# FFN weight differences in the heads of grouped attention, three running sums of probabilities, and denominators placed ahead of the natural-order turn

## The chip, the core and the metric

The program runs on one core of a Trainium2 chip. The core has five engines that run side by side, each in its own order: TensorE (PE, matmuls; PEld is its weight load), VectorE (DVE), ScalarE (ACT), GpSimd (POOL) and SyncE (SP), which here only issues DMAs. They wait for one another through counters (semaphores). The metric is the device time of one execution in microseconds (us). Three runs of the kernel before took 909.49, 909.55 and 912.41 us, so the median is 909.55 us.

## The reference

A perceiver layer on 8 batches of 64 tokens of 512 features (512 tokens in all), in three parts, each added to x:

```python
x = x + xattn(layernorm(x), ctx)   # 16 heads of 32, 1601 context rows per batch, softmax over them
x = x + attn(layernorm(x), ...)    # 32 query heads of 128 in 8 groups of 4, 576 keys, softmax
x = x + ffn(layernorm(x), ...)     # gate and up 512 -> 1792, silu(gate) * up, down 1792 -> 512

def _binary_diff_weight(w, base):  # each of the three FFN weights
    d = w - base
    coeff = jnp.mean(jnp.abs(d))   # one number over all 512 x 1792 elements
    return base + coeff * jnp.sign(d)
```

The mean of |w - base| needs all of w and all of base before the first FFN weight can be made. The change concerns where in the program this mean is gathered.

## The kernel before

**Cross attention** runs over 8 batches `b`. The 1601 context rows are 13 tiles `t` of 128 (the last has 65 rows). In the loop for batch `b`, PE makes scores of batch `b`, the unnormalised values `u` from the exponentials (`values(b, u)`, two tiles at a time), and beside them the scores of batch `b + 1` from which DVE takes row maxima (`max_scores`, `take_max`). ACT makes the exponentials in four buffers `probs`. The denominator of the softmax is the sum of the exponentials over all 13 tiles: POOL adds tiles in pairs into six buffers `sums` (`add_pair`, `add_tail`, seven additions), and PE multiplies the six buffers by a block of ones (`denominators`, twelve matmuls of 512 columns in three rounds of four). At the end of a batch PE's order is: compress the context of batch `b + 3`, turn the maxima, the last `values`, `natural(b + 3)` (a transpose), two score tiles of the next batch, `denominators(b)`. ACT copies the denominators (`copy_den(b - 1)`) after tile 1 of the next batch and before tile 2. In the same loop POOL subtracts three blocks of FFN weights of 896 columns per batch (`difference`) and ACT sums their magnitudes (`abs_sum`, in the array of that name), fed by `load_pieces` on SP's queue. 24 blocks cover all three weight pairs.

**Keys and new tokens** (`rotated_keys`) come next and are not touched.

**Grouped attention** (`attention_and_ffn`) runs 32 heads, `n = 4 g + i`. Heads of groups 1 to 6 stand in a hardware loop. In the pass of head `n`, every engine does this head's scores and exponentials, and the second half of head `n - 1`: PE turns its probabilities (`turn_probs`), ACT copies them to `probs_t_high`, DVE makes `probs_t_low`, PE multiplies by the values (`mix`, which raises `pv`), ACT copies the product to `mixed_t_high`, DVE makes `mixed_t_low` (raises `al`). POOL multiplies each of the head's four probability tiles by the inverse denominator. In the first head of a group (`i = 0`) POOL also waits for `pv` and copies the group's values, and PE runs `output`, 48 matmuls that need `mixed_t_low` from the tenth on. SP loads in each pass the query weight for four heads on, after `wql`, and the output weight for four heads on, after `wol`, which DVE raises in `output_weight_low`. For a group's first head, DVE does `output_weight_low(g, 0)` only in the pass of the second head (`if i == 1`).

**FFN** follows. Before the first head, PE adds the sums over partitions and DVE makes `coeff`; the weights are quantised from the last group on.

The pass of a head, as ACT and DVE have it, and SP's loop stand in full below, with all other functions that the change touches.

## Time and profile before

| | |
|---|---|
| median of 3 runs | 909.55 us |
| the profiled execution | 912.59 us, of it the span of 910.7 us that the profile shows |
| cross attention | 0 to about 295 us |
| keys and new tokens | about 295 to 325 us |
| 32 heads | about 325 to 780 us |
| FFN | about 780 to 911 us |
| PE busy | 866.1 us (95%) |
| DVE, ACT, POOL busy | 609.3, 521.5, 416.2 us |

A timeline row reads: start, duration, engine, line, operation, output<-input with shape, count, and in brackets how long the engine stood idle before it and what released it. Rows that touch in time are merged, so "x4" is four instructions in one row. A matmul's duration contains its way through the array; consecutive ones overlap. A row of windows reads: stretch, its length, then for PE, PEld, DVE, ACT and POOL the busy time and the number of instructions, then the granted clock of TensorE as a share of 2.4 GHz, the busy share of the DMA engines and GB/s.

### The profile page before, as it was taken

The page shows a single profiled execution, that of the slowest core. Times are in us where ns is not written, and L with a number is a line of the kernel's source. Part 1 is how long each engine was busy: PE and PEld are TensorE (multiplying, and loading weights), DVE is VectorE, ACT ScalarE, POOL GpSimd, SP SyncE. Part 2 cuts the span into 40 slices and gives each one's busy share as a digit, 9 for nine tenths or more (in the row PEclk, how much of TensorE's full clock was granted, in tenths as well). Part 3 has the DMA queues.
Part 4 walks back from the last instruction along what each step waited for, and adds up shares of the span by engine and source line. Part 5 has one row for each costly group of instructions (what it writes and reads, how often), then busy time and mean ns, then how long its engine had stood idle before and what let it go on. Part 6 is the DMA issues. An engine that isn't in the chain of part 4 may idle for free.

```text
span 910.7 us, 15512 instructions
## 1 busy us (share of the span) xinstructions
PE 866.1 (95%) x5402; PEld 656.5 (72%) x5402; DVE 609.3 (67%) x994; ACT 521.5 (57%) x1010; POOL 416.2 (46%) x272
## 2 busy tenths in 40 slices
PE   6789999999997989999999999999999999899998
PEld 4444555455442668888888888888888887788886
DVE  4665666576551538858587585876858769768884
ACT  4555666666674547636366373763637647555552
POOL 2397887788876015424244242442424524154430
PEclk9979999999998889999999999999999999999999
DMA  9747664623660721102011020110202003445531
GB/s 365 273 173 290 234 244 145 257 89 113 186 202 1 277 82 47 47 1 70 23 46 46 0 69 23 48 44 8 72 12 67 14 1 113 165 139 189 197 101 47
DMA packets 43202, 102.96 MB, mean 113 GB/s; under 512 B 7954, under 2 KB 13074, under 8 KB 42258
## 3 DMA queue, kind: packets, MB, share of 16 engines
q1 hardware_dynamic: 42866, 102.06, 32.6%
q8 instruction: 30, 0.49, 0.2%
q10 hardware_dynamic: 288, 0.26, 0.1%
q14 instruction: 18, 0.15, 0.1%
HBM read 96.95 MB, written 1.05 MB: 108 GB/s over the span
## 4 chain that ended last, share of the span: by engine, by line
PE 60%; DVE 2%; ACT 1%; DMA 1%; POOL 0%; SPq 0%; issue 0%
PE psum L1356 11%; PE psum L1342 10%; PE psum L1472 8%; PE psum L1410 8%; PE psum L1368 6%; PE psum L1486 4%; PE psum L1395 3%; PE psum L1386 3%; PE psum L1391 3%; PE psum L1377 1%; PE psum L1387 1%; PE psum L1389 1%; DMA ffn_raw<-in_L_ffn_mean_w_dram 1%; POOL ffn_quant L1857 0%; DVE x L1828 0%; DVE norm_stats L162 0%
## 5 line engine op out<-in xcount | busy, mean ns | idle before, releaser
L1844 POOL TENSOR_TENSOR head_probs<-head_probs,inverse_den 128x576 f32<-128x576 f32 x128 | 147.3, 1151 | 273.2 <-DVE inverse_den L1697 273.1
L979 DVE TENSOR_REDUCE max_part<-psum 128x1 f32<-128x804 f32 x128 | 121.2, 990 | 48.3 <-PE psum L693 48.2
L869 ACT ACTIVATE probs<-psum 128x512 f32<-128x512 f32 (+1 forms) x208 | 107.8, 601 | 56.5 <-PE psum L714 48.6
L1579 ACT ACTIVATE head_probs<-psum,neg_max 128x576 f32<-128x576 f32 x128 | 94.7, 740 | 51.2 <-DVE neg_max L1710 50.4
L555 POOL TENSOR_TENSOR prob_sums<-probs 128x1024 f32<-128x1024 f32 x48 | 114.0, 2383 | 19.5 <-ACT probs L869 10.5
L1710 DVE TENSOR_REDUCE neg_max<-psum 128x1 f32<-128x576 f32 x128 | 96.9, 757 | 23.9 <-PE psum L1356 22.7
L1356 PE MATMUL psum<-k_high,query_t_high 128*128 (+1 forms) x256 | 86.7, 339 | 2.0 <-DVE coeff L1783 2.0
L1690 DVE TENSOR_TENSOR probs_t_low<-psum,probs_t_high 128x512 fp32r<-128x512 f32 x124 | 84.8, 684 | 1.0
L714 PE MATMUL psum<-q_t,c_t 97*128 97x512 f32 (+1 forms) x208 | 74.2, 437 | 8.7 <-ACT probs L869 7.0
L693 PEld LDWEIGHTS psum<-c_t,q_t 96*128 96x128 f32 x256 | 43.9, 191 | 50.9 <-DVE max_part L979 29.3
L693 PE MATMUL psum<-c_t,q_t 96*128 96x402 f32 x256 | 75.0, 376 | 5.6 <-DVE max_part L979 3.9
L1368 PE MATMUL psum<-ident,head_probs 128*128 128x128 f32 x496 | 77.9, 273 | 1.6 <-DVE query_t_low L1669 1.4
L1857 POOL TENSOR_TENSOR ffn_quant<-ffn_raw 128x1536 f32<-128x1536 f32 x13 | 45.6, 3508 | 67.6 <-DVE ffn_w_low L1774 26.9
L1356 PE MATMUL psum<-k_high,query_t_low 128*128 (+1 forms) x256 | 76.2, 298 | 0.0
L1356 PE MATMUL psum<-k_low,query_t_high 128*128 (+1 forms) x256 | 76.1, 297 | 0.0
L1585 ACT ACTIVATE probs_t_high<-psum 128x512 fp32r<-128x512 f32 x124 | 72.9, 588 | 0.5 <-PE psum L1377 0.5
L1368 PEld LDWEIGHTS psum<-ident,head_probs 128*128 128x128 f32 x496 | 60.6, 140 | 11.4 <-issue 2.2
L714 PEld LDWEIGHTS psum<-q_t,c_t 97*128 97x128 f32 (+1 forms) x208 | 38.4, 192 | 32.1 <-ACT probs L869 23.0
L1593 ACT ACTIVATE wo_t_high<-wo_nat 128x512 fp32r<-128x512 f32 x32 | 20.0, 626 | 72.4 <-PE psum L1410 72.4
L727 PE MATMUL psum<-probs,c_nat 128*32 128x512 f32 (+1 forms) x416 | 61.0, 621 | 0.0
L1752 DVE TENSOR_TENSOR x<-psum,x 128x512 f32<-128x512 f32 x32 | 22.1, 690 | 46.0 <-PE psum L1410 46.0
L548 POOL TENSOR_TENSOR w_raw<-w_raw 128x896 f32<-128x896 f32 x24 | 50.5, 2105 | 4.3 <-DMA w_raw<-in_L_ffn_mean_w_dram 4.3
(221 smaller groups left out, 1924.3 us busy)
## 6 DMA issues: line engine op xcount, KB each, us to landing
ctx_t_odd<-in_ctx_dram SPq DMA_DIRECT2D x4, 3202.0 KB, 10.7
w_raw<-in_L_ffn_w_dram SPq DMA_DIRECT2D x24, 448.0 KB, 5.3
w_raw<-in_L_ffn_mean_w_dram SPq DMA_DIRECT2D x24, 448.0 KB, 6.4
ffn_raw<-in_L_ffn_w_dram SPq DMA_DIRECT2D x42, 256.0 KB, 3.9
ffn_raw<-in_L_ffn_mean_w_dram SPq DMA_DIRECT2D x42, 256.0 KB, 4.2
cache<-in_ctx_dram SPq DMA_DIRECT2D x3, 3202.0 KB, 10.6
wq_nat<-in_L_attn_wq_dram SPq DMA_DIRECT2D x32, 256.0 KB, 2.9
wo_nat<-in_L_attn_wo_dram SPq DMA_DIRECT2D x32, 256.0 KB, 2.7
```

Source lines behind the costliest of these rows:

```text
L555: pool.tensor_tensor(sums[u][:, :], prob_buffer(b, 2 * u)[:, :], prob_buffer(b, 2 * u + 1)[:, :], ALU.add).then_inc(s_add, 1)
L693: mm = pe.matmul(psum[:, bank + k, 0:PIECE_KEYS], q_t[0:SHIFT, b, 2 * qt:2 * qt + 2, :].rearrange("p h n -> p (h n)"), c_t[0:SHIFT, b % 3, ...
L714: pe.matmul(psum[0:rows_of(t), n % SCORE_BANKS, :], lhs, rhs[:, half * BANK:(half + 1) * BANK], start=True, stop=True).then_inc(s_sb, 1)
L869: act.activation(prob_buffer(b, t)[0:rows, half * BANK:(half + 1) * BANK], psum[0:rows, n % SCORE_BANKS, :], ACT.Exp, scale=XSCALE).then_i ...
L979: dve.tensor_reduce(max_part[:, qt, pair:pair + 1], psum[:, bank:bank + 2, 0:PIECE_KEYS], AX.XY, ALU.max).then_inc(s_max, 1)
L1342: mm = pe.matmul(psum[:, head_bank(i), :], wq_t[a][:, c, :], (xh, xl)[b][:, c, :], start=(k == 0), stop=(k == 3 * DC - 1))
L1356: mm = pe.matmul(psum[:, bank, 0:HALF], q_t[a][:, qt * P:(qt + 1) * P], (k_high, k_low)[b][:, keys], start=(step == 0), stop=(step == 2))
L1368: mm = pe.transpose(bank[:, t * P:(t + 1) * P], probs[:, qt, t * P:(t + 1) * P], core.ident[:, :])
L1579: act.activation(probs[:, qt, :].rearrange("p (a k) -> p a k", a=2), psum[:, 2 * (qt % 2):2 * (qt % 2) + 2, 0:HALF], ACT.Exp, bias=neg_max ...
L1690: dve.tensor_tensor(probs_t[1][:, 0:ST, qt * P:(qt + 1) * P], psum[:, turn_bank(qt), :].rearrange("p (t q) -> p t q", t=ST), probs_t[0][:, ...
L1710: dve.tensor_reduce(neg_max[:, qt:qt + 1], psum[:, 2 * (qt % 2):2 * (qt % 2) + 2, 0:HALF], AX.XY, ALU.max, negate=True).then_inc(s["max"], 1)
L1844: pool.tensor_tensor(probs[:, qt, :], probs[:, qt, :], rden[:, qt:qt + 1].to_broadcast([P, KEYS]), ALU.mult).then_inc(s["norm"], 1)
```

## The change

Three things move.

1. **The FFN weight blocks leave cross attention.** `load_pieces`, `difference` and `abs_sum` are gone from it. In grouped attention the weights are cut into 28 pieces of 256 columns, one per head of the first seven groups. In pass `n` SP first waits for `s_abs >= 3n + 1`, issues the six DMAs of piece `n` (`load_piece`) and only then goes to the query weight and the output weight. POOL, after the head's four tiles (and in `i = 0` after the values), adds the last piece's three sums to `total`, waits for all six DMAs, and subtracts the blocks in the order 1, 2, 0. ACT sums the magnitudes of blocks 1 and 2 in the same pass, ahead of the copy to `mixed_t_high`, and those of block 0 in the next pass, ahead of the first exponential. `coeff` is made in head 28 and no longer before head 0.
2. **Three running sums in cross attention.** POOL adds tile by tile into three buffers (tiles 0 to 3, 4 to 7, 8 to 12), ten additions for a batch in place of seven; two sets alternate between batches.
3. **`denominators` takes the place of the last `values`**, ahead of `natural(b + 3)` and the next batch's scores. It holds the last tile's two value matmuls and six matmuls of the sums (twelve before), the last four of them after POOL's last addition.

```diff
-PIECE = WSIZE // P // BATCH
+PIECE = WSIZE // P // (NH - REP)
...
+SUM_OF = {1: 0, 2: 0, 3: 0, 5: 1, 6: 1, 7: 1, 9: 2, 10: 2, 11: 2, 12: 2}
...
+            def add_tile(b, t):
+                rows = slice(0, rows_of(t))
+                total = sums[3 * (b % 2) + SUM_OF[t]]
+                first = t - 1 not in SUM_OF
+                pool.wait_ge(s_exp, HALVES * b + 2 * t + 2)
+                if first:
+                    wait(pool, s_den, b - 1)
...
+                pe.wait_ge(s_exp, HALVES * (b + 1))
+                pe.wait_ge(s_add, SUMMED * b + 3)
+                for half in range(2):
+                    at = 2 * LKV * half
+                    mm = pe.matmul(psum[at:at + LKV, U_BANK, :], c_nat[0:TAIL, b % 3, KT - 1, :],
+                                   prob_buffer(b, KT - 1)[0:TAIL, half * BANK:(half + 1) * BANK], start=False, stop=True)
+                    add_up(half, 1, 0, True, False)
+                mm.then_inc(s_pv, 1)
+                pe.wait_ge(s_add, SUMMED * (b + 1))
+                for half in range(2):
+                    add_up(half, 0, 1, True, True)
+                    mm = add_up(half, 1, 2, False, True)
                 mm.then_inc(s_den, 1)
...
+                    sp.wait_ge(s_abs, 3 * (REP * (g - 1) + i) + 1)
+                    load_piece(REP * (g - 1) + i)
+                    stand_alone(sp, core)
                     wait(sp, s["wql"], REP * (g - 1) + i + 1)
                     load_query_weight(core, qo, sp, g, i)
...
                 early_weights(g, i)
+                for k in range(1, 3):
+                    abs_sum(g, i, k)
                 if last:
                     act.wait_ge(s["pv"], n)
                     act.activation(mixed_t[0][:, (i - 1) % REP, :], psum[:, head_bank(i), :], ACT.Copy).then_inc(s["ah"], 1)
...
+            def piece(g, i):
+                n = REP * g + i
+                if not (isinstance(g, int) and (g == 0 and i == 0 or g == NKV - 1 and i > 0)):
+                    pool.wait_ge(s_abs, 3 * n + 1)
+                    pool.tensor_tensor(total[:, :], total[:, :], part[:, :], ALU.add).then_inc(s_tot, 1)
+                if isinstance(g, int) and g == NKV - 1:
+                    return
+                pool.wait_ge(s_piece, 96 * (n + 1))
+                for k in (1, 2, 0):
+                    pool.tensor_tensor(slot[:, k, 0, :], slot[:, k, 0, :], slot[:, k, 1, :],
+                                       ALU.subtract).then_inc(s_pdiff, 1)
```

SP's queue in the loop over heads, one pass, before; `query_weight_low_done` is `wql`, `output_weight_low_done` is `wol`:

```order
L298 ISA [waits query_weight_low_done]
L298 DMA wq_nat<-in_L_attn_wq_dram 128x512
L303 DMA wo_nat<-in_L_attn_wo_dram 128x512 [waits output_weight_low_done,first_stage_reached]
L74 REGISTER_ALU
L298 ISA [waits query_weight_low_done]
```

and now, from the end of one pass into the next:

```order
L302 DMA wo_nat<-in_L_attn_wo_dram 128x512 [waits output_weight_low_done,first_stage_reached]
L1301 ISA
L1296 ISA [waits w_piece_abs_done]
L1296 DMA w_piece<-in_L_ffn_w_dram 128x256
L1296 DMA w_piece<-in_L_ffn_mean_w_dram 128x256
L1296 DMA w_piece<-in_L_ffn_w_dram 128x256
L1296 DMA w_piece<-in_L_ffn_mean_w_dram 128x256
L1296 DMA w_piece<-in_L_ffn_w_dram 128x256
L1296 DMA w_piece<-in_L_ffn_mean_w_dram 128x256
L74 REGISTER_ALU [waits first_stage_reached]
L297 ISA [waits query_weight_low_done]
L297 DMA wq_nat<-in_L_attn_wq_dram 128x512
```

The six DMAs of a piece stand behind the output weight of the pass before, and so behind its wait for `wol`.

ACT at the end of a head's pass and the start of the next, before:

```order
L1593 ACTIVATE wo_t_high<-wo_nat 128x512 [waits output_weight_in1]
L1571 ACTIVATE mixed_t_high<-psum 128x512 [waits head_mix_done]
L1585 ACTIVATE probs_t_high<-psum 128x4x128 [waits head_probs_turned]
L1579 ACTIVATE head_probs,den<-psum,neg_max 128x576 [waits head_probs_turned,head_max_done]
L1585 ACTIVATE probs_t_high<-psum 128x4x128 [waits head_probs_turned]
```

and now:

```order
L1597 ACTIVATE wo_t_high<-wo_nat 128x512 [waits output_weight_in2]
L1576 ACTIVATE w_piece,abs_part<-w_piece 128x256 [waits w_piece_diff_done] x2
L1566 ACTIVATE mixed_t_high<-psum 128x512 [waits head_mix_done]
L1589 ACTIVATE probs_t_high<-psum 128x4x128 [waits head_probs_turned]
L1576 ACTIVATE w_piece,abs_part<-w_piece 128x256 [waits w_piece_diff_done]
L1583 ACTIVATE head_probs,den<-psum,neg_max 128x576 [waits head_probs_turned,head_max_done]
```

Two magnitude sums that wait for POOL stand ahead of `mixed_t_high`, one ahead of the first exponential.

PE at the end of a batch of cross attention, before:

```order
L727 MATMUL psum<-probs,c_nat 32x512 [waits probs_done]
L727 MATMUL psum<-probs,c_nat 32x512
L663 MATMUL psum<-ident,c_parts 128x128 [waits c_parts_copied]
L663 MATMUL psum<-ident,c_parts 128x128 x2
L664 MATMUL psum<-ident,c_parts 65x32
L714 MATMUL psum<-q_t,c_t 128x512 [waits shift_row_done,probs_done]
L714 MATMUL psum<-q_t,c_t 128x512 [waits probs_done] x3
L744 MATMUL psum<-prob_sums,ones_by_latent 32x512 [waits prob_pairs_summed,values_placed]
L744 MATMUL psum<-prob_sums,ones_by_latent 32x512 x3
L744 MATMUL psum<-prob_sums,ones_by_latent 32x512 [waits prob_pairs_summed]
```

and now:

```order
L720 MATMUL psum<-probs,c_nat 32x512 [waits prob_pairs_summed,probs_done,c_parts_copied]
L713 MATMUL psum<-prob_sums,ones_by_latent 32x512
L720 MATMUL psum<-probs,c_nat 32x512
L713 MATMUL psum<-prob_sums,ones_by_latent 32x512
L713 MATMUL psum<-prob_sums,ones_by_latent 32x512 [waits prob_pairs_summed]
L713 MATMUL psum<-prob_sums,ones_by_latent 32x512 x3
L634 MATMUL psum<-ident,c_parts 128x128 [waits c_parts_copied]
L634 MATMUL psum<-ident,c_parts 128x128 x2
L635 MATMUL psum<-ident,c_parts 65x32
L687 MATMUL psum<-q_t,c_t 128x512 [waits shift_row_done,probs_done]
```

The denominators come ahead of the transposes and the next scores, in two rounds of four; the second waits for POOL's last addition.

## Rows read from the trace of the kernel before

**Rows 1.** The page: busy shares, and the chain that ended last by engine.
```profile
PE 866.1 (95%) x5402; PEld 656.5 (72%) x5402; DVE 609.3 (67%) x994; ACT 521.5 (57%) x1010; POOL 416.2 (46%) x272
...
PE 60%; DVE 2%; ACT 1%; DMA 1%; POOL 0%; SPq 0%; issue 0%
```

**Rows 2.** Timeline at the end of a batch of cross attention.
```profile
208.02 2.78 PE L744 MATMUL psum<-prob_sums,ones_by_latent 128*32 128x512 f32 x24
...
210.86 1.20 ACT L899 ACTIVATE u_all<-psum 64x512 f32<-64x512 f32 x2 [1.87 <-PE psum L744]
...
212.09 2.06 ACT L869 ACTIVATE probs<-psum 128x512 f32<-128x512 f32 x4
```

**Rows 3.** Waits, 30 to 130 us (in total, times, longest).
```profile
ACT probs L869 <- POOL prob_sums L555: 4.1, 2, 2.4
```

**Rows 4.** Groups of POOL's instructions by shape (busy, mean ns).
```profile
L555 POOL TENSOR_TENSOR prob_sums<-probs 128x1024 f32<-128x1024 f32 x48 | 114.0, 2383 | 19.5 <-ACT probs L869 10.5 <-PE psum L744 9.0
L548 POOL TENSOR_TENSOR w_raw<-w_raw 128x896 f32<-128x896 f32 x24 | 50.5, 2105 | 4.3 <-DMA w_raw<-in_L_ffn_mean_w_dram 4.3
...
L569 POOL TENSOR_TENSOR c_low<-c_parts,c_high 128x449 fp32r<-128x449 f32 x7 | 8.0, 1147 | 22.2 <-ACT c_high L883 22.2
```

**Rows 5.** Timeline at the first head.
```profile
333.85 0.40 PE L1356 MATMUL psum<-k_high,query_t_high 128*128 128x288 f32 x1 [1.97 <-DVE coeff L1783]
```

**Rows 6.** Timeline, third head of a group: end of one pass, start of the next.
```profile
430.88 1.15 POOL L1844 TENSOR_TENSOR head_probs<-head_probs,inverse_den 128x576 f32<-128x576 f32 x1 [0.36 <-DVE inverse_den L1697]
...
433.70 0.60 ACT L1571 ACTIVATE mixed_t_high<-psum 128x512 fp32r<-128x512 f32 x1 [1.54 <-PE psum L1395]
...
435.83 0.68 DVE L1690 TENSOR_TENSOR probs_t_low<-psum,probs_t_high 128x512 fp32r<-128x512 f32 x1
...
436.66 0.62 PE L1368 MATMUL psum<-ident,head_probs 128*128 128x128 f32 x4
```

**Rows 7.** Groups of ACT's instructions by shape.
```profile
L892 ACT ACTIVATE w_raw<-w_raw 128x896 f32<-128x896 f32 x24 | 22.7, 952 | 0.0
...
L250 ACT ACTIVATE new_tokens<-psum 128x256 f32<-128x256 f32 x1 | 0.4, 383 | 0.9 <-PE psum L241 0.9
```

**Rows 8.** Line 1665, its durations (ns, min/median/max).
```profile
L1665 DVE TENSOR_TENSOR wq_t_low<-wq_nat,wq_t_high x32: 683/806/984, 326.4 to 746.5; 128x512 fp32r<-128x512 f32 x32
```

**Rows 9.** Timeline, first head of a group.
```profile
445.11 0.60 ACT L1571 ACTIVATE mixed_t_high<-psum 128x512 fp32r<-128x512 f32 x1 [2.11 <-PE psum L1395]
445.26 0.61 POOL L1834 CAST value_high<-cache 128x512 fp32r x1 [1.82 <-PE psum L1395]
...
445.82 0.30 POOL L1835 CAST value_high<-v_new 128x128 fp32r x1
...
446.95 0.39 PE L1410 MATMUL psum<-wo_t_high,mixed_t_high 128*128 128x512 f32 x1
```

**Rows 10.** Timeline, second head of a group.
```profile
464.49 1.15 POOL L1844 TENSOR_TENSOR head_probs<-head_probs,inverse_den 128x576 f32<-128x576 f32 x1 [0.36 <-DVE inverse_den L1697]
...
466.92 0.33 SPq L303 DMA_DIRECT2D wo_nat<-in_L_attn_wo_dram  x1
...
467.32 0.60 ACT L1571 ACTIVATE mixed_t_high<-psum 128x512 fp32r<-128x512 f32 x1 [1.54 <-PE psum L1395]
...
470.27 0.60 PE L1368 MATMUL psum<-ident,head_probs 128*128 128x128 f32 x4
```

**Rows 11.** The page's DMA issues (KB each, us to landing).
```profile
ffn_raw<-in_L_ffn_mean_w_dram SPq DMA_DIRECT2D x42, 256.0 KB, 4.2
...
wo_nat<-in_L_attn_wo_dram SPq DMA_DIRECT2D x32, 256.0 KB, 2.7
```

**Rows 12.** SP's queue in time, one issue of a row of such.
```profile
260.58 0.43 SPq L494 DMA_DIRECT2D w_raw<-in_L_ffn_w_dram  x1
```

**Rows 13.** Windows around the start of the heads.
```profile
325.00:327.00 2.00, 0.00 (x0) 0.00 (x0) 0.82 (x2) 1.04 (x3) 0.41 (x2) 1.00 0.16 18
327.00:331.00 4.00, 3.80 (x10) 3.02 (x11) 0.06 (x1) 0.00 (x0) 0.00 (x0) 0.57 0.83 306
```

More of the change, by code:

```diff
@@ L327, with sums_after @@
 C_WIDTH = MAIN + TAIL
-DIFF_AT = (0, 1, 2)
-ABS_AT = 3
+SUM_OF = {1: 0, 2: 0, 3: 0, 5: 1, 6: 1, 7: 1, 9: 2, 10: 2, 11: 2, 12: 2}
+SUMMED = len(SUM_OF)
+def sums_after(t):
+    return sum(1 for i in SUM_OF if i <= t) + (t + 1 in SUM_OF and t not in SUM_OF)
 COMPRESS_BANK = (4, 3, 6) + (4,) * (BATCH - 3)
@@ L855, in _ @@
                     scores(b + 1, 1)
-                denominators(b)
             mix(BATCH - 1)
```

131 lines of the change are left out of this document (56 added, 75 removed).

## The prediction

> **What bounds the kernel now.** I read the page first. PE is busy 95% of the span and alone holds 60% of the chain that ended last; DVE has 2%, ACT and DMAs 1% each, POOL nothing [rows 1]. So work taken from ACT or POOL is worth only what PE waits for them, and work or waits added to them cost what PE then waits. I then went to the places that the change touches, in time. In cross attention a batch hangs at its end on denominators and ACT, inside on DVE's maxima and PE by turns. In the heads PE runs without a gap, and ACT, DVE and POOL have short waits between its steps. I cost the two stages apart.
>
> **Cross attention: the end of a batch.** Before, the denominators are 24 records (12 matmuls, two passes each) that take 2.78 us, three rounds of four side by side, about 0.86 us a round. ACT waits 1.87 us for them, copies in 1.20 us and starts tile 2 at 212.09 [rows 2]. Now the last value matmuls share a round with the first sum, and one round follows: two rounds less. But these rounds now stand ahead of the transposes and the next scores, so ACT's next exponentials start one round (0.86 us) later, and its wait of 1.87 us goes. Tile 2 starts 1.87 - 0.86 = 1.0 us earlier. The rest of the batch hangs on tile 2 and moves with it. Five batches (0 to 4) compress a context at the end, which gives POOL 3.4 us to finish its additions: 5 x 1.0 = 5.0 us.
>
> POOL has ten additions of 2.38 us for a batch instead of seven and three differences of 2.10 [rows 4]: 23.8 against 23.0 us. Counted from the start of tile 2, its last addition ends at 22.7 us in the new order. With the compress PE comes to its second wait at 24.0, without one at 21.4. So at the ends of batches 5 and 6 PE waits about 1.4 us, and with the round ahead of the scores the gain is gone: I take a loss of 0.15 us each, 0.3 together. The last batch is POOL's before and after (24.2 against 23.8 us of additions, then the same last round): a gain of 0.1.
>
> Batch 0: ACT waits twice for POOL's sums, 4.1 us together [rows 3], since the first difference stands ahead of the first addition. In the new order the additions keep ahead of the four buffers, and the units fall back to DVE's pace of 3.35 us; I take 1.6 us, bounded by 0 and 4.1.
>
> The first score of head 0 waits 1.97 us for `coeff` [rows 5]. Without that it waits for the low query part, which ends 0.7 us earlier: 0.7 us. The product in head 28 stands among 48 matmuls; POOL's `total` is ready 1 us after `mix`, the matmul asks for it 8 us after. Nothing.
>
> Gain of this side: 5.0 + 1.6 - 0.3 + 0.1 + 0.7 = 7.1 us (bounds 3 and 14: all of two rounds in each of eight ends). The removed 22 MB of weight traffic and ACT's sums had cover, I take nothing for them.
>
> **The heads, one piece's prices.** POOL's two-input operations cost 1.147 us at 449 columns and 2.105 at 896 [rows 4], so 2.14 ns a column and 0.19 fixed: 0.73 us for 256 (bounds 0.65 and 0.85), and about 0.1 for the 3-column sum. ACT's magnitude sum is 0.952 at 896; a copy of 256 columns is 0.383 [rows 7]. I take 0.40 to the next instruction.
>
> **Third and fourth heads of a group.** POOL ends the head's last tile at 430.88 + 1.15 = 432.03 [rows 6]. Sum 0.1, then block 1 to 432.9, block 2 to 433.6, ACT's second sum to 434.1. The copy to `mixed_t_high`, which now stands behind it, was at 433.70 [rows 6]: 0.4 us late. From it hang `mixed_t_low`, the next row maximum, and `probs_t_low` at 435.83, which ends 0.15 us before PE's turn at 436.66 needs it [rows 6]. So PE waits about 0.27 us. 14 such heads: 3.8 us. Block 0's sum, ahead of the first exponential, falls into ACT's wait of 1.1 us for the maximum there: nothing.
>
> `wq_t_low`, with two SBUF inputs, takes 0.683 us alone and 0.806 in the middle beside POOL's multiplication, 0.984 at most [rows 8], while that one takes 1.15 us throughout [rows 6]. The Trainium skill (SBUF — State Buffer, "SBUF: two separate sides") says that such a VectorE operation and a GpSimd operation hold the shared ports exclusively, and that the later one blocks fully until the first ends. By that the output weight's low part and the two differences would queue, 0.7 us more in each of these 14 heads, and the sum would be 10 us higher; the rows show a slowdown by 0.1 to 0.3 us and I keep to them.
>
> **First head of a group.** Here the piece stands behind the values, which wait for `pv`. POOL is free at 445.82 + 0.30 = 446.12 [rows 9]. Sum 446.2, blocks 446.95 and 447.7, ACT's second sum 448.15. `mixed_t_high` was at 445.11 [rows 9]. It is 3.0 us late, ends 448.75; `mixed_t_low` ends 449.5. PE needs it at its tenth matmul, at 446.95 [rows 9]. It waits 2.6 us. Groups 1 to 6 have both halves (head 0 has no `mix`, head 28 no differences): 6 x 2.6 = 15.6 us.
>
> **Second head of a group.** SP's queue is in order. Its output-weight DMA waits for `wol`, and the count for a group's first head is raised only late in the pass of the second: the row stands at 466.92 [rows 10]. The six DMAs of the second head's piece are now behind it. The first begins at 467.5, an issue takes 0.43 us [rows 12], so the sixth begins at 469.7. Landing takes 2.7 us for 256 KB by itself and 4.2 in a burst of six [rows 11]; a piece's block is 128 KB, so I take 2.7: 472.4. POOL, free since 465.64 [rows 10], ends blocks 1 and 2 at 473.9, ACT's sum ends at 474.35. `mixed_t_high` was at 467.32 [rows 10]: 7.0 us late. Behind this copy on ACT stand all copies and exponentials of the next head, behind POOL's wait its scaling. PE can do two tiles of the third head and then stands: its turn at 470.27 [rows 10] comes 6.9 us later. Seven groups (heads 1, 5, ... 25): 48.3 us. The later pieces are in time: the third head's is issued after its block 0, at about 476.0, and landed by 481.2, while POOL wants it at 483.7.
>
> The Trainium skill (DMA: Bandwidth & Descriptors, "Anatomy of one DMA") gives, for a DMA issued by GpSimd, a fixed cost of about 2.0 us and the bytes over 436 GB/s, so by estimate 2.3 us for a block. With that the seven waits would be 2.8 us shorter in all; no row shows a block of 128 KB.
>
> **TensorE's clock.** After PE stood still from 325 to 327 us the granted clock fell: 0.57 over the 4 us that follow, that is 3.4 us at 1.2 instead of 2.4 GHz [rows 13]. That costs 1.7 us of PE's work. I charge it to all seven long waits (11.9 us) and to half of the six of 2.6 us (5.1 us). Bounds: nothing, and twice that much at each.
>
> **Sum.** 48.3 + 15.6 + 3.8 + 11.9 + 5.1 - 7.1 = 77.6 us more. The profiled execution took 912.6 us, 1.7 of them outside its span of 910.7, and 3.0 more than the median of 909.55. On the execution 990, on the median 987 us. Own range: with short landings and no clock loss +50, with landings of 4.2 us and twice the clock loss +115: 960 to 1025.
>
> **The rivals.**
> - *The clock stays low.* Each of 13 waits is followed by twice 3.4 us at half clock, as wherever PE's work after a gap is thin. For it: 327 us shows one such stretch per gap, with PE dense. Against: the matmuls after a head's wait are dense too. 13 x 3.4 in place of 17.0: +27, so 1014 us.
> - *The second head's piece comes in time*, because the output weight's wait does not hold SP as I read it. Then its wait of 6.9 us becomes the 0.27 of the others: 909.55 + 15.6 + 5.1 + 5.7 - 7.1 = 929 us. Against: 466.92 is right behind DVE's low part, and nothing else explains that DMA's time.
> - *Faster.* The gain of cross attention stands alone. It decides at one point: ACT must finish both sums before `pv`. The time from POOL's last tile to the copy is 1.67 us (432.03 to 433.70) [rows 6], and the steps need 2.1 with the piece in place. If POOL's short operations cost half of what the slope says and `mixed_t_high` had slack in the first heads too, the result is 909.55 - 7.1 = 902 us. Against: in the first head of a group the work starts after `pv` by construction, so 15.6 us stay.
>
> **How the numbers follow.** Forecast 0.77, clock 0.10, in time 0.08, faster 0.03, something near no change 0.02. The likeliest gives 987 us. The range 958 to 1014 reaches the clock's case and leaves out the case in time. A measurement of this kernel tells 0.3% (2.7 us) from no change. Every case but the last two is slower by more: faster 0.03, same 0.02, slower 0.95.
>
> **What would show it.** At the end of a batch with a compress, tile 2 starts 1 us nearer to the tile before it, and a batch takes 29.3 instead of 30.35 us; the last two ends show PE waiting for `prob_sums`. In the heads ACT's longest waits are those of the magnitude sums for `w_piece`, with seven near 8 us; POOL waits for the piece's DMA seven times, about 7 us each, in second heads only; PE's waits come in three sizes, 7, 2.6 and 0.3 us, and the clock is at half after the long ones. A group takes 56.2 us now and about 69 after. The forecast is wrong if POOL never waits for `w_piece`, if a group still takes under 60 us, or if PE's wait in `output` is absent.

## Result and profile after

The changed kernel takes 1027.07 us (median of 6 runs, 1024.10 to 1030.18), the kernel before 909.52 us (6 runs, 905.17 to 914.00). The ratio is 1.1292, 95% interval 1.1264 to 1.1320: 117.5 us slower. The prediction said 987 us, 77.5 more, with a range of 958 to 1014. The sign was right, and so was the mechanism in the heads; in cross attention the sign was wrong, and in all 40 us are missing.

The profiled execution took 1024.10 us, its span is 1022.2 us, 111.5 more than before. The page after, where it answers to [rows 1, 4, 7]: busy shares, the granted clock of TensorE in 40 slices, the chain that ended last, and the groups of POOL's subtractions, ACT's magnitude sums and PE's first products behind the long wait (busy, mean ns, idle before).

```profile
PE 890.3 (87%) x5306; PEld 669.0 (65%) x5306; DVE 608.0 (59%) x993; ACT 533.9 (52%) x1130; POOL 503.0 (49%) x385
...
PEclk9889999999779989979979999899899899999999
...
PE 28%; issue 21%; POOL 11%; DVE 3%; ACT 1%; DMA 1%; SPq 0%; POOLq 0%; DVEq 0%; ACTq 0%
...
L1330 PE MATMUL psum<-attn_x_high,wq_t_high 128*128 128x512 f32 x128 | 50.8, 442 | 52.3 <-DVE mixed_t_low L1686 49.6
...
L1576 ACT ACTIVATE w_piece<-w_piece 128x256 f32<-128x256 f32 x84 | 35.0, 416 | 115.4 <-POOL w_piece L1867 115.4
...
L1867 POOL TENSOR_TENSOR w_piece<-w_piece 128x256 f32<-128x256 f32 x84 | 65.8, 810 | 52.6 <-DMA w_piece<-in_L_ffn_mean_w_dram 52.6
```

PE's share of the chain fell from 60% to 28%, POOL's rose from 0 to 11%. The seven waits of POOL for the piece and of PE for `mixed_t_low` are there. New is that PE's 24 us more of busy time are not more work (it has 96 matmul records fewer): ten of the 40 slices of the clock row are below 9, where the kernel before has four.

So I divided the span at two marks (the last denominators, and PE's first query product). "PE stands" is the length of a part less PE's busy time in it. "Lost at half clock" is half of PE's busy time inside the stretches whose granted clock is 0.50:

| us | before | after | more |
|---|---|---|---|
| start to the last denominators | 290.6 | 300.1 | 9.5 |
| of it PE stands / lost at half clock | 25.8 / 9.5 | 38.7 / 21.9 | 12.9 / 12.4 |
| keys and new tokens | 36.6 | 36.1 | -0.5 |
| heads and FFN | 583.5 | 686.0 | 102.5 |
| of it PE stands / lost at half clock | 11.3 / 3.4 | 86.3 / 22.0 | 75.0 / 18.6 |

In cross attention the two add up to more than 9.5 us because PE also has fewer matmuls to do there. In the heads they leave some 9 of the 102.5 us that I can't assign.

The prediction had -6.4 in the first row and +84 in the heads. Cross attention misses by 16 us, the heads by 18.

**A batch's end in cross attention.** Timeline of PE and ACT of the kernel after at the place of [rows 2].

```profile
205.61 1.11 PE L674 MATMUL psum<-ident,max_row 128*97 128x128 f32 x8
...
207.12 1.45 PE L713 MATMUL psum<-prob_sums,ones_by_latent 128*32 128x512 f32 x9
...
209.15 0.96 PE L687 MATMUL psum<-q_t,c_t 97*128 97x512 f32 x3
...
211.78 1.20 ACT L874 ACTIVATE u_all<-psum 64x512 f32<-64x512 f32 x2
213.00 1.09 ACT L849 ACTIVATE probs<-psum 128x512 f32<-128x512 f32 x2
213.03 0.63 PE L666 MATMUL psum<-c_t,q_t 96*128 96x402 f32 x2 [1.22 <-ACT u_all L874]
...
214.08 1.77 PE L741 MATMUL psum<-wv_u,u_all 128*64 128x33 f32 x32
215.78 1.94 PE L700 MATMUL psum<-probs,c_nat 128*32 128x512 f32 x8
```

From the turn of the maxima to tile 2 it is now 7.39 us; before it was 8.37 (203.72 to 212.09). The 1.0 us forecast is there. ACT no longer waits for the denominators. But PE now stands for 1.22 us where it stood for 0.29, and behind that the next two steps take 1.77 and 1.94 us. In the kernel before the same three places read:

```profile
212.12 0.63 PE L693 MATMUL psum<-c_t,q_t 96*128 96x402 f32 x2 [0.29 <-ACT u_all L899]
...
213.17 1.12 PE L760 MATMUL psum<-wv_u,u_all 128*64 128x33 f32 x32
214.22 1.06 PE L727 MATMUL psum<-probs,c_nat 128*32 128x512 f32 x8
```

The windows of the stretch after (the granted clock is the third number from the right):

```profile
213.00:214.00 1.00, 0.97 (x4) 0.67 (x4) 0.29 (x1) 1.00 (x3) 1.00 (x1) 1.00 0.21 54
214.00:216.00 2.00, 2.00 (x37) 1.83 (x40) 0.81 (x2) 1.07 (x3) 1.86 (x2) 0.58 0.25 62
216.00:217.60 1.60, 1.60 (x8) 0.00 (x0) 0.94 (x3) 0.00 (x0) 1.46 (x2) 0.50 0.25 62
217.60:220.00 2.40, 2.40 (x14) 1.79 (x10) 1.66 (x2) 1.43 (x3) 1.61 (x1) 0.97 0.19 45
```

The clock falls to 1.2 GHz once a batch and costs 1.5 us, more than the 1.0 gained. A batch takes 30.9 us, not 29.3. Such a stretch follows the gap at five of six batches; behind the sixth, a gap of 1.21 us at 244.0, there is none.

At batches 5 and 6 PE stands 2.04 and 2.32 us for POOL's last addition, and half-clock stretches of 3.4 and 10.2 us follow. At the end of the last batch PE stands for POOL once more:

```profile
298.14 1.93 PE L713 MATMUL psum<-prob_sums,ones_by_latent 128*32 128x512 f32 x8 [5.15 <-POOL prob_sums L536]
```

The distances between the mixes show where the time went. The first mix comes 1.3 us earlier than before. The next four batches take 30.9 us in place of 30.3 or 30.4, in sum 2.2 us more. The last three take 31.0, 29.1 and 27.3 in place of 27.3, 27.4 and 24.2, in sum 8.5 us more.

**The second head of a group.** POOL, SP's queue, ACT and PE of the kernel after, in the stretch that answers to [rows 10].

```profile
503.73 0.64 POOL L1862 TENSOR_TENSOR abs_total<-abs_total,abs_part 128x3 f32<-128x3 f32 x1
505.06 0.33 SPq L302 DMA_DIRECT2D wo_nat<-in_L_attn_wo_dram  x1
505.67 0.33 SPq L1296 DMA_DIRECT2D w_piece<-in_L_ffn_w_dram  x1
...
508.05 0.33 SPq L1296 DMA_DIRECT2D w_piece<-in_L_ffn_mean_w_dram  x1
...
511.70 2.09 POOL L1867 TENSOR_TENSOR w_piece<-w_piece 128x256 f32<-128x256 f32 x3 [7.33 <-DMA w_piece<-in_L_ffn_mean_w_dram]
...
513.55 0.58 ACT L1566 ACTIVATE mixed_t_high<-psum 128x512 fp32r<-128x512 f32 x1
...
515.00 1.19 PE L1330 MATMUL psum<-attn_x_high,wq_t_high 128*128 128x512 f32 x2 [6.88 <-DVE mixed_t_low L1686]
```

The steps are those of the forecast: the piece's six issues stand right behind the output weight, POOL waits for the last landing, ACT for POOL, and PE for `mixed_t_low`. PE's seven waits sum to 49.6 us (48.3 forecast). The last block lands 3.65 us after its issue where 2.7 was assumed, so that the two sums agree so closely is in part luck.

**Third head.** POOL and DVE at the end of a pass, and PE's wait behind it; it answers to [rows 6, 8].

```profile
524.26 1.15 POOL L1848 TENSOR_TENSOR head_probs<-head_probs,inverse_den 128x576 f32<-128x576 f32 x1 [0.36 <-DVE inverse_den L1701]
525.15 0.80 DVE L1669 TENSOR_TENSOR wq_t_low<-wq_nat,wq_t_high 128x512 fp32r<-128x512 f32 x1
525.36 0.65 POOL L1862 TENSOR_TENSOR abs_total<-abs_total,abs_part 128x3 f32<-128x3 f32 x1
525.87 0.68 DVE L1705 TENSOR_TENSOR wo_t_low<-wo_nat,wo_t_high 128x512 fp32r<-128x512 f32 x1
525.97 2.57 POOL L1867 TENSOR_TENSOR w_piece<-w_piece 128x256 f32<-128x256 f32 x3
...
528.29 0.58 ACT L1566 ACTIVATE mixed_t_high<-psum 128x512 fp32r<-128x512 f32 x1
...
531.00 0.63 PE L1356 MATMUL psum<-ident,head_probs 128*128 128x128 f32 x4 [0.56 <-DVE probs_t_low L1694]
```

POOL's addition of three numbers takes 0.65 us and ends with DVE's `wq_t_low` (526.01 and 525.95). The three subtractions take 2.57 us beside `wo_t_low`. In a first head, where DVE has nothing of the kind in hand, the same two take 0.19 and 2.11 us. Taken singly, the first of the three subtractions has 1.18 us in third and fourth heads and 0.74 in first heads; the other two have about 0.73 in both.

```profile
552.72 0.19 POOL L1862 TENSOR_TENSOR abs_total<-abs_total,abs_part 128x3 f32<-128x3 f32 x1
552.87 2.11 POOL L1867 TENSOR_TENSOR w_piece<-w_piece 128x256 f32<-128x256 f32 x3
```

The copy to `mixed_t_high` starts 2.88 us after POOL's last tile ends, before 1.67, forecast 2.1. What a head costs is seen best in the distance of these copies from pass to pass (us; the names are those of the head in whose pass the copy stands):

| copy to the next copy | before | after | late `wo` | and ACT late |
|---|---|---|---|---|
| fourth head to first | 11.4 | 14.1 | 14.1 | 11.4 |
| first to second | 22.2 | 30.0 to 31.9 | 23.5 or 25.1 | 22.2 |
| second to third | 11.3 | 13.4 to 14.7 | 12.3 | 11.5 |
| third to fourth | 11.3 | 12.3 | 12.3 | 11.3 |

The last two columns are experiments below. The third heads show a price of 1.0 us where the prediction had 0.27. A group takes 70.3 to 71.7 us from copy to copy, where the prediction had about 69.

### The profile page after: what moved, and what is told of

Same layout as the page of the kernel before. It is cut to its first block, busy times and chain, and to the rows that moved or that the text cites. A ratio compares the mean times of both kernels' runs of the same rounds, so it can differ in the third digit from the quotient of the medians.

```text
span 1022.2 us, 16044 instructions
## 1 busy us (share of the span) xinstructions
PE 890.3 (87%) x5306; PEld 669.0 (65%) x5306; DVE 608.0 (59%) x993; ACT 533.9 (52%) x1130; POOL 503.0 (49%) x385
## 4 chain that ended last, share of the span: by engine, by line
PE 28%; issue 21%; POOL 11%; DVE 3%; ACT 1%; DMA 1%; SPq 0%; POOLq 0%; DVEq 0%; ACTq 0%
PE psum L1467 8%; POOL head_probs L1848 5%; POOL w_piece L1867 4%; PE psum L1344 4%; PE psum L1330 4%; PE psum L1481 4%; PE psum L1356 3%; PE psum L1383 1%; PE psum L1374 1%; PE psum L1379 1%; DVE probs_t_low L1694 1%; PE psum L1398 1%; POOL abs_total L1862 1%; PE psum L1365 1%; DMA ffn_raw<-in_L_ffn_mean_w_dram 0%
## 5 line engine op out<-in xcount | busy, mean ns | idle before, releaser
L536 POOL TENSOR_TENSOR prob_sums<-prob_sums,probs 128x1024 f32<-128x1024 f32 (+1 forms) x56 | 133.4, 2383 | 8.5 <-ACT probs L849 0.5
L1330 PE MATMUL psum<-attn_x_high,wq_t_high 128*128 128x512 f32 x128 | 50.8, 442 | 52.3 <-DVE mixed_t_low L1686 49.6
L1686 DVE TENSOR_TENSOR mixed_t_low<-psum,mixed_t_high 128x512 fp32r<-128x512 f32 x31 | 21.4, 691 | 125.4 <-ACT mixed_t_high L1566 125.4
L1576 ACT ACTIVATE w_piece<-w_piece 128x256 f32<-128x256 f32 x84 | 35.0, 416 | 115.4 <-POOL w_piece L1867 115.4
L1356 PE MATMUL psum<-ident,head_probs 128*128 128x128 f32 x496 | 82.7, 284 | 12.1 <-DVE probs_t_low L1694 10.1
L1867 POOL TENSOR_TENSOR w_piece<-w_piece 128x256 f32<-128x256 f32 x84 | 65.8, 810 | 52.6 <-DMA w_piece<-in_L_ffn_mean_w_dram 52.6
L1344 PE MATMUL psum<-k_high,query_t_high 128*128 (+1 forms) x256 | 89.1, 348 | 1.9 <-DVE query_t_low L1673 1.4
L1356 PEld LDWEIGHTS psum<-ident,head_probs 128*128 128x128 f32 x496 | 62.4, 146 | 29.3 <-issue 21.9
L687 PE MATMUL psum<-q_t,c_t 97*128 97x512 f32 (+1 forms) x208 | 76.6, 452 | 4.0 <-ACT probs L849 2.9
L536 POOL TENSOR_TENSOR prob_sums<-probs 128x1024 f32<-128x1024 f32 x24 | 57.1, 2381 | 29.8 <-ACT probs L849 29.7
## 6 DMA issues: line engine op xcount, KB each, us to landing
ctx_t_odd<-in_ctx_dram SPq DMA_DIRECT2D x4, 3202.0 KB, 11.3
```

What stands on the lines that cost most here:

```text
L536: pool.tensor_tensor(total[rows, :], (prob_buffer(b, t - 1) if first else total)[rows, :], prob_buffer(b, t)[rows, :], ALU.add).then_inc(s ...
L1330: mm = pe.matmul(psum[:, head_bank(i), :], wq_t[a][:, c, :], (xh, xl)[b][:, c, :], start=(k == 0), stop=(k == 3 * DC - 1))
L1344: mm = pe.matmul(psum[:, bank, 0:HALF], q_t[a][:, qt * P:(qt + 1) * P], (k_high, k_low)[b][:, keys], start=(step == 0), stop=(step == 2))
L1356: mm = pe.transpose(bank[:, t * P:(t + 1) * P], probs[:, qt, t * P:(t + 1) * P], core.ident[:, :])
L1867: pool.tensor_tensor(slot[:, k, 0, :], slot[:, k, 0, :], slot[:, k, 1, :], ALU.subtract).then_inc(s_pdiff, 1)
```

## The experiments

Time is the median, the ratio is to the kernel before measured beside it, with its 95% interval. The kernels without pieces and the one without the addition to `total` leave out the mean of the weight differences; they put a constant in its place. "Cross" is the time of the last denominators in the profile, "heads" the remaining two parts without the keys (before 290.6 and 583.5, after 300.1 and 686.0).

| kernel | us | ratio | cross | heads |
|---|---|---|---|---|
| late `wo` | 972.3 | 1.0688 (1.0657 to 1.0718) | 306.1 | 629.2 |
| last round back | 999.6 | 1.0984 (1.0961 to 1.1007) | 278.6 | 682.7 |
| no pieces | 922.3 | 1.0132 (1.0105 to 1.0158) | 305.5 | 580.2 |
| no pieces, filled | 913.5 | 1.0038 (1.0018 to 1.0058) | 296.2 | 580.8 |
| late `wo`, ACT late | 929.5 | 1.0242 (1.0204 to 1.0279) | 299.9 | 587.2 |
| all three | 902.1 | 0.9927 (0.9903 to 0.9952) | 278.3 | 585.6 |
| filled heads | 1019.3 | 1.1215 (1.1170 to 1.1260) | 305.2 | 673.2 |
| denominators ahead only | 931.3 | 1.0239 (1.0209 to 1.0269) | 309.5 | 583.9 |
| last round back, no pieces | 899.6 | 0.9875 (0.9847 to 0.9904) | 280.9 | 580.9 |
| weights stay | 948.8 | 1.0438 (1.0399 to 1.0477) | 328.4 | 582.6 |
| weights stay, ACT late | 952.8 | 1.0460 (1.0413 to 1.0508) | 330.8 | 584.0 |
| no addition to `total` | 963.1 | 1.0576 (1.0547 to 1.0604) | 305.9 | 619.6 |

**1. Late output weight.**

```diff
-                    wait(sp, s["wol"], REP * (g - 1) + i + 1)
-                    load_output_weight(core, qo, sp, g, i)
+                    for j in ((), (0, 1), (2,), (3,))[i]:
+                        wait(sp, s["wol"], REP * (g - 1) + j + 1)
+                        load_output_weight(core, qo, sp, g, j)
```

> The changed kernel with one thing moved on SP's queue: a group's first output weight is loaded in the pass of the second head, behind that head's piece, so the piece no longer stands behind the wait for wol. Theory A (queue position): POOL's seven long waits for the piece (52.6 us in all) and PE's seven waits of about 7.1 us (49.6 us) become about 0.6 us each, that is 45.5 us less, and the half-clock stretches around them (PE busy 29.9 us in them, so 14.9 us lost) go to nearly nothing, 13 us less: 1027 - 58 = about 969 us (960 to 978). Theory B (the piece lands late because six DMAs of 128 KB take long, wherever they stand): PE's seven waits stay above 5 us and the time above 1010 us. Clock theory apart: if the clock loss hung on something else than these waits, the time would be about 982 us.

972.3 us. The seven waits of PE are gone, the heads 56.8 us shorter. It was the place in SP's queue. Of that PE's standing time is 42.9 us and the work lost at half clock 15.2 us. Cross attention, which this edit doesn't touch, ends at 306.1 here and at 300.1 in the trace after: the half-clock stretches between 238 and 293 us fell differently (16.5 us lost against 6.3). Four kernels with the same code there end at 305 to 306, two at 300. That the median after lies 3 us over its profiled execution fits with this; the other executions have no trace that would show it.

**2. Last round of denominators behind the next scores.**

```diff
                 mm.then_inc(s_pv, 1)
-                pe.wait_ge(s_add, SUMMED * (b + 1))
-                ...
                     scores(b + 1, 1)
+                last_round(b)
```

> The changed kernel with the last round of denominators (the four matmuls that wait for POOL's last addition) moved behind the next batch's first two score tiles; the last values and the first sum stay ahead. Theory A (a gap of 1.22 us on PE at each batch's head takes the clock to half for 3.4 us, 1.5 to 1.7 us of work a batch, which eats the 1.0 us gained; at batches 5 and 6 PE stands 2.0 and 2.3 us for POOL): the round fills the gap, ACT starts tile 2 0.8 us earlier, the half-clock stretches at batches 1 to 6 go: 5 x 2.4 + 2 x 2.7 = 17 us less, about 1010 us (1006 to 1016). Theory B (cross attention is slower because POOL's ten dependent additions hold ACT's buffers all through the batch): the period stays near 30.9 us, time 1023 to 1028 us.

999.6 us, 27.5 less, more than expected. PE in this kernel at a batch's end:

```profile
198.31 0.50 PE L687 MATMUL psum<-q_t,c_t 97*128 97x512 f32 x1 [0.22 <-ACT probs L857]
198.75 1.06 PE L728 MATMUL psum<-prob_sums,ones_by_latent 128*32 128x512 f32 x8
...
201.14 0.64 PE L666 MATMUL psum<-c_t,q_t 96*128 96x402 f32 x2 [0.29 <-ACT u_all L882]
...
202.19 1.12 PE L748 MATMUL psum<-wv_u,u_all 128*64 128x33 f32 x32
203.24 1.07 PE L700 MATMUL psum<-probs,c_nat 128*32 128x512 f32 x8
```

The gap is 0.29 again, the mix takes 1.12 us, and the mean clock from 60 to 240 us is 1.00. A batch takes 28.6 us, with the same ten additions on POOL, so these don't hold the batches before the last. In the last one they do: PE still stands 5.16 us for POOL at 276.7. Cross attention ends at 278.6, 12.0 us before that of the kernel before, nearly twice the gain that I had forecast for the whole change there.

**3 and 4. No pieces, and no pieces with the gap filled.** The second adds five matmuls that nobody reads:

```diff
+                    if b > 0 and u == 0:
+                        pe.wait_ge(s_u, 2 * b)
+                        for _ in range(5):
+                            pe.matmul(psum[:, U_BANK, :], c_t[0:STACK, b % 3, 0:P], ...)
```

> The changed kernel without any of the weight pieces: no piece DMA, no difference, no magnitude sum, the coefficient is made from a constant (left out: the mean of the weight differences). What is left is the change in cross attention and the place of the coefficient. By the prediction on record this is 909.5 - 7.1 = 902.4 us. By the clock theory (in cross attention 5.8 us of PE's work more is lost at half clock before the keys, and PE waits for POOL at batches 5 to 7): the last round of denominators ends 9 us later than before, the stage of the keys is 1 to 2 us longer, so 919 to 921 us, with the half-clock stretches of 3.4 us at each of batches 1 to 6 and no wait over 2.5 us in the heads.

> As the kernel without pieces, and in each batch from 1 on five matmuls of 97x512 more, whose result nobody reads, at the place where PE stands for 1.22 us (between the third score tile and the second maxima). Work is added, the wait of the others is unchanged. Clock theory: the granted clock stays at 1.00 behind that place in batches 1 to 4 and the next steps (the mix of 32 matmuls, eight value matmuls) take 1.12 and 1.06 us instead of 1.77 and 1.94: 5 to 6 batches x 1.5 us = 7 to 9 us less than without them, about 912 us. If the clock is a by-product and not the cause, the time is the same or up to 2 us longer, 919 to 923 us.

922.3 and 913.5 us. The change in cross attention alone is 11 us slower than the kernel before, not 7 faster. In the traces cross attention is 14.9 us longer and the heads 3.3 shorter; nothing is lost at half clock in these heads, where the kernel before loses 3.4 us. With more work in the gap it is 8.8 us faster than without. Windows of the two from 60 or 62 to 230 us, first without, then with the added matmuls:

```profile
60.00:230.00 170.00, 161.30 (x1230) 88.28 (x1226) 107.29 (x136) 93.17 (x174) 139.97 (x62) 0.95 0.32 110
```

```profile
62.00:230.00 168.00, 163.78 (x1278) 90.86 (x1277) 110.91 (x141) 94.59 (x175) 145.30 (x65) 1.00 0.34 115
```

The wait of PE for `u_all` and all other work stayed, and work was added, so the lower clock is a cause of the longer time and no by-product.

**5. Late output weight, and ACT's sums behind `mixed_t_high`.**

```diff
-                for k in range(1, 3):
-                    abs_sum(g, i, k)
                 if last:
                     act.wait_ge(s["pv"], n)
                     act.activation(mixed_t[0][:, (i - 1) % REP, :], ...
+                for k in range(1, 3):
+                    abs_sum(g, i, k)
```

> The kernel with the late output weight (972.3 us), and ACT's two magnitude sums of blocks 1 and 2 moved behind the copy to mixed_t_high in every head. Theory A (the sums ahead of the copy are what delays mixed_t_low in first, third and fourth heads): PE's six waits of 2.33 us in output go (14.0 us), its waits of 0.45 to 0.6 us, three or four in a group, go (7 x 1.6 = 11 us), and the three half-clock stretches of the heads behind them (5.1 us): 972 - 30 = about 942 us (936 to 950). Theory B (POOL and its shared access to memory slow DVE, so mixed_t_low is late anyway): PE's waits of 2.33 us stay above 1.5 us and the time stays above 962 us.

929.5 us, 42.8 less where 30 were expected. In the traces the heads are 42.0 us shorter: PE stands 29.6 us less and 3.4 us less are lost at half clock; the other 9 us I can't assign. All waits of PE in the heads of the kinds 2.33 and 0.56 us are gone, and the heads are within 3.7 us of before. So these costs reached PE through the place of ACT's sums ahead of the copy. POOL's slow operations remain but PE no longer waits for them.

**6. All three.**

> All three: the late output weight, the magnitude sums behind mixed_t_high, and the last round of denominators behind the next scores. If the causes add up, the gain of the third (27.5 us) comes on top of the second's 942: about 914 us; if what is left of the pieces in the heads without any wait is under 5 us, it is 922.3 - 27.5 + 5 = about 900 us. I take 907 us (898 to 917), so within 1% of the kernel before (910 us).

902.1 us, 0.73% faster than the kernel before (small, but its interval leaves out 1) and 12% faster than the change. The parts of its page:

```profile
PE 849.6 (94%) x5306; PEld 647.4 (72%) x5306; DVE 615.3 (68%) x993; ACT 531.1 (59%) x1130; POOL 510.5 (57%) x385
...
PEclk9879999999996999999999999999999999999999
```

**7. The long wait in third heads filled.**

```diff
                             pe.wait_ge(s["wql"], n + 2)
+                            if i == 2 and not (isinstance(g, int) and g == NKV - 1):
+                                for _ in range(7):
+                                    pe.matmul(psum[SEQ:P, head_bank(i), :], core.x[:, 0, 0:SEQ], core.x[:, 0, :], ...)
                             wait(pe, s["al"], n - 1)
```

> The changed kernel, and in each third head of groups 0 to 6 seven matmuls of 64x512 in plain 32 bits more, whose result nobody reads, just ahead of PE's long wait for mixed_t_low (0.85 us each by estimate, so about 6 of its 7.1 us are filled with work). The wait of ACT and DVE for the piece is unchanged. Clock theory: the granted clock stays at 1.00 behind the seven long waits, and the 2.0, 2.7, 3.2, 1.7, 1.7, 1.8 and 1.8 us (14.9 us) of work lost in these stretches are not lost: 1027 - 14 = about 1013 us (1009 to 1018). If the clock falls because of the short waits of 2.3 us ahead of them, or the filler overruns the wait, 1024 to 1032 us.

1019.3 us. In the heads only three stretches of 3.4 us at half clock are left (5.1 us lost, not 22.0), and the heads are 12.8 us shorter, as the clock theory says. The whole is only 7.8 us faster, outside the range that I had expected; in its trace cross attention ended at 305.2, which takes back 5 us. Windows ahead of the wait's end and behind it, after:

```profile
507.90:515.00 7.10, 0.22 (x2) 0.03 (x1) 0.83 (x2) 2.37 (x8) 2.09 (x3) 0.74 0.52 161
515.00:521.40 6.40, 6.33 (x24) 5.36 (x25) 3.96 (x8) 4.22 (x11) 2.29 (x2) 0.50 0.57 164
```

and in the filled kernel:

```profile
511.40:517.60 6.20, 6.18 (x15) 1.79 (x14) 0.04 (x1) 1.58 (x6) 2.10 (x3) 1.00 0.60 186
517.60:521.50 3.90, 2.58 (x17) 2.14 (x18) 3.61 (x7) 3.36 (x9) 1.15 (x1) 1.00 0.45 124
```

**8. The kernel before with its three rounds ahead.**

```diff
                 values(b, UNITS - 1)
+                denominators(b)
                 if b + 3 < BATCH:
                     natural(b + 3)
                 ...
                     scores(b + 1, 1)
-                denominators(b)
```

> The kernel before with one thing of the change: all three rounds of denominators, of the old six sums, ahead of the natural-order turn and of the next scores; the weight blocks stay where they were. Theory A (it is the order that opens PE's gap, not the number of sums): three rounds take 2.58 us and ACT's wait of 1.87 us goes, so tile 2 starts 0.7 us later, PE's gap there grows from 0.29 to about 1.2 us and the clock falls once a batch, 1.5 us more: six or seven batches x 2.2 = 13 to 15 us more than 909.5, so about 923 us (918 to 930), with a stretch at half clock in most batches. Theory B (the gap comes of the new sums alone): at most 6 x 0.7, 910 to 914 us, no stretch at half clock between 60 and 270 us.

931.3 us. The kernel also carries the waits that this order needs, and DVE's `copy_u` ahead of `place_values`, as in the change. PE at the place of the gap:

```profile
191.82 1.03 PE L695 MATMUL psum<-c_t,q_t 96*128 96x402 f32 x2 [1.22 <-ACT u_all L901]
```

PE's gap there is 1.22 us at six batches, and the stretches at half clock are 6.8 us long in place of 3.4. The order opens the gap, with the old sums too, and in this kernel it costs about 3 us a batch. The size was just above my range.

**9. Last round back, no pieces.**

> The kernel with the last round behind the next scores, without any weight pieces (left out: the mean of the weight differences). It gives what the pieces still cost in the heads once nothing waits for them: the kernel with all three edits takes 902.1 us, the one without pieces and with the denominators ahead 922.3, and the last round moved back gave 27.5. If these add, 894.8 us (891 to 898), and the pieces cost 7 us. If the pieces are free once their waits are gone, 901 to 903 us.

899.6 us. Once nothing waits for them the pieces cost 2.5 us by the medians (902.1 - 899.6), but 4.7 us by the two ratios (0.9927 and 0.9875) and 4.7 us in the heads of the two traces. So the price lies between "free" and the 7 us expected.

**10 and 11. The weights stay in cross attention**, with three sums and the last round behind the scores; in the second, ACT's last two sums of a batch stand behind the copies of the compressed context.

```diff
                 for t in SUM_OF:
+                    if t in (5, 9, 11):
+                        difference(b, (5, 9, 11).index(t))
                     add_tile(b, t)
```

> The kernel before with the three sums and the last round behind the next scores, but with the three weight differences of 896 columns left in cross attention (ahead of tiles 5, 9 and 11), none in the heads. Theory A (POOL's work per batch decides: ten additions of 2.38, three differences of 2.10 and the low part of 1.15 us are 31.3 us, against a batch of 28.6 us when POOL is not the bound): each batch takes at least 31.3 us, seven batches x 2.7 = 19 us more than without them, so 895 + 19 to 25 us = 914 to 920 us, slower than the kernel before. Theory B (the differences fit into POOL's idle time, so moving the weights was not needed): 895 to 900 us.

> The kernel whose weights stay in cross attention (948.8 us), with ACT's second and third magnitude sums moved behind the copies of the compressed context, so that PE's last values and denominators no longer wait for them (PE stood 15.3 us, five times, for c_parts, and the clock fell behind each). Theory A (POOL's work of 31.3 us a batch decides once that wait is gone): a batch takes 31.3 to 32 us instead of 33 to 34, five waits of 3 us and part of 30 us of lost clock go: 915 to 928 us, still slower than the kernel before. Theory B (only ACT's order was wrong, POOL's load is harmless): 898 to 905 us. If POOL alone already set the 33.7 us: above 940 us.

948.8 and 952.8 us. Both forecasts were too low; in the second only the last case named, POOL alone sets the pace, has the right number. In the first, a batch takes 32.6 to 35.7 us: PE stands 2.8 to 3.3 us for `c_parts` at five ends.

```profile
186.34 0.62 PE L756 MATMUL psum<-probs,c_nat 65*32 65x512 f32 x1 [2.75 <-ACT c_parts L900]
```

In the second that wait is gone, but PE stands 1.66 us or more for ACT's exponentials, behind two magnitude sums of 0.93 us, and at four ends 1.6 to 2.6 us for POOL's last addition. In both, up to 20 us in a row are at half clock. POOL is busy 31 us a batch in both (windows of the first):

```profile
182.50:215.50 33.00, 29.94 (x237) 15.93 (x234) 19.53 (x25) 19.70 (x37) 31.03 (x15) 0.95 0.34 103
```

So the ten additions and the old differences don't fit together in a batch of 28.6 us. How much of the 49 us above the kernel of experiment 9 is POOL's load and how much is the clock behind the waits stays open.

**12. No addition to `total`.** The twelfth kernel is the late output weight without POOL's 28 additions.

> The kernel with the late output weight (972.3 us), without POOL's 28 additions of three numbers to abs_total (left out: the sum over the pieces, so the mean of the weight differences). These additions take 0.19 us in the seven first heads and 0.64 us in all others, where they stand beside VectorE's wq_t_low and end within 0.1 us of it (526.01 and 525.95). Theory A (the addition is not slow, it waits until VectorE's operation gives the memory free, and the first subtraction behind it waits in the same way for wo_t_low): without it the first subtraction takes its place and waits instead, the heads get at most 0.2 us shorter each, 968 to 973 us, and the three subtractions take more than 2.57 us together. Theory B (0.64 us is what a small POOL operation costs there): every second, third and fourth head's copy to mixed_t_high comes 0.6 us earlier, 20 x 0.6 = 12 us less, 958 to 963 us, the subtractions as long as before.

963.1 us, as theory B's number has it, but the rows are those of theory A. From copy to copy second to fourth heads take 12.15 us in place of 12.30: 0.15 less, not 0.6. POOL and DVE in a third head of this kernel:

```profile
505.64 0.81 DVE L1670 TENSOR_TENSOR wq_t_low<-wq_nat,wq_t_high 128x512 fp32r<-128x512 f32 x1
505.86 3.03 POOL L1869 TENSOR_TENSOR w_piece<-w_piece 128x256 f32<-128x256 f32 x3
506.37 1.22 DVE L1706 TENSOR_TENSOR wo_t_low<-wo_nat,wo_t_high 128x512 fp32r<-128x512 f32 x1
```

The subtractions grew from 2.57 to 3.03 us, and now `wo_t_low`, which in third heads used to take 0.68, takes 1.22: it had to wait for POOL's. The rest of the 9.2 us lies in the step from a first to a second head (22.9 us in place of 23.5) and in a few us of clock; why that step gains more is not resolved.

## Why the prediction came out as it did

- **Second heads, 48.3 us: right.** Measured 49.6; moving one DMA in SP's queue took the waits away (experiment 1). The landing was assumed at 2.7 us. The median of all blocks is 2.4 or 2.5, but the last of the six that POOL waits for took 3.65; what made up for it was not separated.
- **First heads, 15.6 us: nearly.** PE's wait in `output` is 2.33 us six times, 14.0. By the distances of the copies a first head has 3 us of its own, some 18 in all.
- **Third and fourth heads, 3.8 us: wrong, 14.** This step failed: "Sum 0.1, then block 1 to 432.9, block 2 to 433.6". The sum takes 0.64 us there and the first block about 1.2, because DVE's `wq_t_low` and `wo_t_low` run at that moment; the slope of [rows 4] holds only without them (2.11 us for three blocks in first heads). Each head is 1.0 us longer, not 0.27. Experiment 5 adds that PE pays this only because ACT's sums stand ahead of the copy. I had the other reading in hand and set it aside: the Trainium skill (SBUF — State Buffer, "SBUF: two separate sides") says that the later of the two fully waits. The trace agrees with 0.64 us in place of 0.19 and 1.18 in place of 0.74. By it I had put 10 us more on the sum, and 14 x (1.0 - 0.27) is 10.2. I had laid all of it on `wo_t_low`; the trace has half of it at the addition beside `wq_t_low`. What misled me was [rows 8], probably because DVE's operation met multiplications of POOL that were partly over; that was not tried by itself. Experiment 12 shows the wait in both directions: POOL's three subtractions take 3.03 us there against 2.11 alone, DVE's 1.22 against 0.68.
- **The clock in the heads, 17.0 us: right in sum** (18.6 measured), though the count was coarse. The stretches in first heads cost 1.7 us in three groups and nothing in the others, the long waits 1.7 to 3.2 each, 15.2 where I had 11.9; the kernel before loses 1.7 us behind its wait for `coeff` that this one doesn't. Experiment 7 took most of it away while the piece came as late as before.
- **Cross attention, 6.4 us gained: wrong sign, 9.5 to 15 lost.** The step that failed is "Tile 2 starts 1.87 - 0.86 = 1.0 us earlier", taken five times as a gain of 5.0 us with nothing against it. The 1.0 us came, but I priced PE's new gap at nothing. The three rounds that I took out of ACT's way had been what PE did while ACT made two exponentials and the copy. I charged the clock to the waits of the heads and not to this one. In the trace after, the clock costs 12.4 us more than before (experiments 2, 4 and 8 show cause and place). That is not all. The miss of 16 us has about 6 at the four steady batches, 1 before them, and 8 in the last three. The waits at batches 5 and 6 were 2.04 and 2.32 us where I had 1.4, and the clock fell behind them. And "The last batch is POOL's before and after", with its gain of 0.1, was wrong: POOL needs 26.4 us there (271.65 to 298.09), not 23.8. It stands 1.6 us of that for ACT's exponentials, just behind a stretch in which PE ran at half clock (268.9 to 279.2), and this batch costs 3.1 us more than before. How this splits between the clock and the ten additions stays open.
- **Sum of the miss.** Cross attention 16, third and fourth heads 10, first heads 2, long waits and clock of the heads 3, the first group's start and waits that the rows don't separate some 3. That is 34, the miss between the profiled executions. The other 6 us are how these lie to their medians: the one before 3 above, the one after 3 below.
- **The rivals.** None of them hit the time. "The clock stays low" gave 1014 with the right kind of cause, but the cost that was missing lay in the other stage. In the heads the stretches around the long waits are indeed 6.8 or 10.2 us long, but PE stands in part of them, so they cost less than the rival had. The piece came as late as read, and POOL's short operations were dearer, not cheaper.

## What to carry to other kernels

Work that is taken out of the way of a waiting engine may have been the filling of PE's gap: before moving it, read what PE does in that time, and charge the half-clock stretch as a likely cost to every new gap of PE that is longer than those the trace shows to be harmless. Here 0.29 us always was; 1.22 was not in five of six cases, and one gap of 1.46 us at 84.0 had no stretch behind it up to the next gap at 89.5. Look at the last rounds of a loop apart: there a wait that was covered inside may lie open. A DMA added to an in-order queue belongs ahead of any wait that is raised late, and a helper's sum on ACT belongs behind the copy for which PE waits. The price of a small operation on GpSimd is that of the moment: look at what VectorE does with two operands in SBUF at the same time.

## What the runs showed of the hardware

- A gap of PE of 1.22 us, once in 30.9 us, with PE dense on both sides, was followed by 3.4 us at 1.2 GHz in five of six batches; gaps of 0.29 us were not. In the heads a gap of 2.33 us was followed by such a stretch in three groups and by none in three.
- Five matmuls more a batch made a kernel 8.8 us faster (922.3 to 913.5).
- The same code of cross attention ended at 300 us in two traces and at 305 to 306 us in four. The mean granted clock from 238 to 293 us was 0.88 in the trace after and 0.69 in that of experiment 1.
- GpSimd's addition of 128x3 took 0.19 us alone and 0.64 beside a VectorE subtraction of 128x512 with both operands in SBUF; VectorE's subtraction took 0.68 us when it came first and 1.22 when GpSimd's subtraction of 128x256 came first.
